# Query, key and value projection of a decoder layer as three rounded passes with two new helpers on VectorE and GpSimd

## The chip, the cores and the metric

The kernel runs on one core of a Trainium2 chip. The metric is device time in microseconds for one launch. The kernel is written without a scheduler: each engine's queue is written out by hand, and the engines meet at semaphores.

## The reference, cut to what matters

A post-norm decoder layer on 128 x 64 tokens of width 128, in three blocks, then a mixture-of-experts block. The change touches the first:

```python
Xn  = _layernorm(X, ln_g, ln_b)
QKV = jnp.einsum('bsd,ed->bse', Xn, W_in)        # 128 -> 384
Q, K, V = jnp.split(QKV, 3, axis=-1)
Q, K = _rotary(Q, ROT), _rotary(K, ROT)
A = jnp.sum(_l2norm(K) * V, axis=-2)
Y = jnp.einsum('bsd,ed->bse', A[:, None, :] * _l2norm(Q), W_out)
# x = _layernorm(x + Y + X); then cross attention with 16 heads of 64,
# layer norm, top-2 routing over 8 experts, expert FFN, layer norm
```

## The kernel before

The 8192 tokens are 64 tiles of 128 rows. The program has three stages: a prologue that prepares weights and takes the first five tiles through the projection, a loop of periods in which all blocks up to the routing run interleaved (period `t` scores tile `t`, projects tile `t+5`, and finishes tiles `t-1` to `t-5`), and then the expert FFN and the closing norm, which don't change.

A period has four units, `k` = 0 to 3. The order of every engine in a unit is written by hand in the function `period` of that engine; waits on semaphores do the rest. In each unit TensorE scores one (batch, half of the heads) pair (L1367), ScalarE takes exponentials (L698) after VectorE has found the maxima (L945), VectorE inverts the sums (L951), GpSimd scales the probabilities (L513), and one unit later TensorE turns them (L1390), ScalarE rounds them (L707), VectorE takes the rests (L956), and TensorE weighs (L1401 to L1404) in three passes of the rounded type `float32r`: high x high, high x low, low x high.

The projection of tile `t+5` goes through these steps, in units 1 and 2 of a period:

- VectorE normalises the rows, `x_hat` (L863);
- TensorE turns them into PSUM, `turn_x` (L1427, unit 1, into columns 384 to 511 of the bank `ps_a`);
- ScalarE applies gain and bias on the way out of PSUM, `x_turned` (L657), giving `xnT`, 128 x 128 in float32;
- TensorE multiplies, `make_qkv` (L1431, unit 2): one float32 instruction of 384 columns, `xnT` stationary and `winT` moving. The profile shows a float32 matmul as two records, a `float32r` matmul as one;
- ScalarE copies the result out, `keep_qkv` (L664), and squares queries and keys (L666), GpSimd makes the inverse roots (`qk_rstds`, L505 and L507), and VectorE rotates (L875 to L885) and multiplies keys by values (L893), after which TensorE turns the queries (L1436).

In the prologue the same functions stand in a written sequence for tiles 0 to 4 between the weight jobs `prepare(0)` to `prepare(14)` (L1348 to L1355); tiles 0 to 4 alternate between `ps_a` and `ps_o`. `winT` is made once by ScalarE (L645) out of the bank `ps_s[0]`, columns 0 to 383; columns 384 to 511 there become `woutT` (L646).

GpSimd's queue in unit 1 is: scale (L513), `ctx_hat` (L546), `latent_hat` (L552), and the indirect DMA that routes rows of an earlier tile (L525); unit 2 begins with the next scale.

Of the kernel before, what the change touches and what calls it, by code (L numbers as in the profile page):

```python
# [14 lines left out]
def decoder_layer(nc, x, ctx_in, w_in, w_out, ln_g, ln_b, ln1_g, ln1_b, ln2_g, ln2_b,  # L15
                  w_q, w_kv, w_o, expert_w, w_g, b_g, rot_cos, rot_sin, batch_of, eye,
                  before, expert_ids, region_base, row_ids, tile_ids, x_rows, y_rows, out):
    F32 = mybir.dt.float32
# [8 lines left out]
    P = 128  # L27
# [35 lines left out]
    with ctx:  # L63
# [20 lines left out]
        b_lat = sb("b_lat", [P, 1])  # L84
        winT = sb("winT", [P, 3 * D])
        woutT = sb("woutT", [P, D])
# [23 lines left out]
        c_hat = sb("c_hat", [P, 2, D])  # L110
        xnT = sb("xnT", [P, 2, D])
        qkv = sb("qkv", [P, 2, 3 * D])
# [161 lines left out]
        def U_BANK(n):  # L274
# [18 lines left out]
        c_in = [sem(f"c_in{q}") for q in range(X_RING)]  # L293
        names = """in_stats in_moments in_eps in_rstd x_hat_done c_hat_done xT_ps xnT_done qkv_ps qkv_done sq_done
        qk_eps qk_rstd rot_turned rot_cosed rot_done kvp_done pick_done at_ps yT_done wo_ps 
# [6 lines left out]
        e_sum_done e_z_done e_stats e_moments e_eps e_rstd e_nm_done e_out_done""".split()  # L302
        (in_stats, in_moments, in_eps, in_rstd, x_hat_done, c_hat_done, xT_ps, xnT_done, qkv_ps, qkv_done, sq_done,
         qk_eps, qk_rstd, rot_turned, rot_cosed, rot_done, kvp_done, pick_done, at_ps, yT_done, wo_ps, 
# [183 lines left out]
        def _(pool):  # L488
# [49 lines left out]
            def qk_rstds(j):  # L538
                q = j % 2
                rstd(ss_qk[:, q], se_qk[:, q], rs_qk[:, q], eps_l2, sq_done, 2 * j + 2, qk_eps, qk_rstd, j)  # L540

            def ctx_hat(j):
                q = j % 2
                pool.wait_ge(in_rstd, j + 1)
                pool.wait_ge(kvT_ps, count(j - 1))
                nc.gpsimd.tensor_scalar(c_hat[:, q], c_raw[:, j % X_RING], mv_in[:, q, 1, 0:1], rs_in[:, q, 1:2],  # L546
                                        ALU.subtract, ALU.mult).then_inc(c_hat_done, 1)
# [7 lines left out]
            def period(t, c):  # L555
                p = c % 2
                for k in range(UNITS):
# [11 lines left out]
                    if k == 1 and on(t, 4):  # L569
                        latent_hat(t + 4)  # L570
                    if k == 2 and on(t, 5):
                        qk_rstds(t + 5)
# [8 lines left out]
            ctx_hat(0)  # L581
            ctx_hat(1)
            qk_rstds(0)
            qk_rstds(1)
            in_rstds(2)
# [3 lines left out]
            latent_hat(1)  # L589
            in_rstds(3)  # L590
            qk_rstds(2)
            ctx_hat(2)
            ctx_hat(3)
            z1_rstds(2)
# [3 lines left out]
            z1_rstds(3)  # L598
            latent_hat(3)
            ctx_hat(4)  # L600
            qk_rstds(4)
# [29 lines left out]
        def _(act):  # L631
# [8 lines left out]
            def keep_prepared(at):  # L640
# [3 lines left out]
                if kind == "in":  # L644
                    nc.scalar.activation(winT[:], bank[:, 0:3 * D], ACT.Copy).then_inc(win_kept, 1)  # L645
                    nc.scalar.activation(woutT[:], bank[:, 3 * D:4 * D], ACT.Copy, scale=0.5).then_inc(prep_act, 1)  # L646
                elif kind == "t":
                    nc.scalar.activation(dst, bank[:], ACT.Copy).then_inc(prep_act, 1)
                elif kind == "m":
                    nc.scalar.activation(heads_of(g, score_hi[:]), bank[:].rearrange("p (c d) -> p c d", c=4), ACT.Copy,  # L650
                                         scale=QS_SCALE).then_inc(prep_act, 1)
                else:
                    nc.scalar.activation(dst, bank[:].rearrange("p (c d) -> p c d", c=4), ACT.Copy).then_inc(prep_act, 1)

            def x_turned(j):
                act.wait_ge(xT_ps, j + 1)
                nc.scalar.activation(xnT[:, j % 2], A_XT(j), ACT.Identity, scale=gcol[:, 0:1],  # L657
                                     bias=bcol[:, 0:1]).then_inc(xnT_done, 1)
# [169 lines left out]
        def _(dve):  # L828
# [32 lines left out]
            def in_hats(j):  # L861
                dve.wait_ge(in_rstd, j + 1)
                nc.vector.tensor_scalar(x_hat[:, j % 2], x_raw[:, j % X_RING], mv_in[:, j % 2, 0, 0:1], rs_in[:, j % 2, 0:1],  # L863
                                        ALU.subtract, ALU.mult).then_inc(x_hat_done, 1)

            def qk(j):
# [70 lines left out]
            def period(t, c):  # L937
# [165 lines left out]
                if on(t, 0):  # L1103
                    row_max(2)
                if on(t, 2):
                    rows_low(t + 2)
# [62 lines left out]
            keep_prepared(1)  # L1169
            in_hats(1)  # L1170
            dve.wait_ge(s_lat, 64)
            nc.vector.tensor_scalar(g_lat[:], g_lat[:], (1 + EPS_LN) ** -0.5, None, ALU.mult).then_inc(g_lat_set, 1)
# [15 lines left out]
            keep_prepared(8)  # L1188
            stats(3)
            x1_norm(1)  # L1190
            in_hats(3)
            rotate(2)
            keep_prepared(9)
# [15 lines left out]
            residual(3)  # L1209
            rows_low(1)  # L1210
            dve.wait_ge(s_gate, 32)
            dve.wait_ge(s_place, 64)
# [111 lines left out]
        def _(pe):  # L1324
# [104 lines left out]
            def make_qkv(j):  # L1429
                pe.wait_ge(xnT_done, j + 1)  # L1430
                nc.tensor.matmul(A_QKV(j), xnT[:, j % 2], winT[:], start=True, stop=True).then_inc(qkv_ps, 1)  # L1431

# [81 lines left out]
            prepare(1)  # L1514
            pe.wait_ge(win_kept, 1)
            make_qkv(0)
# [176 lines left out]
```

## Time and profile before

| what | us |
|---|---|
| median of 3 runs | 1526.59 (1523.41 to 1527.76) |
| profiled execution | 1525.28 |
| its span | 1523.4 |
| PE busy in the span | 1378.8 |
| ACT busy | 1147.2 |
| DVE busy | 1129.9 |
| POOL busy | 902.7 |

PE is TensorE, ACT ScalarE, DVE VectorE, POOL GpSimd. The profile divides the span in 40 slices; the loop of periods fills most of them, the expert FFN and the closing norm the last ten. A row of the timeline gives an instruction's start and length; lengths of matmuls contain the time through the array, so neighbouring matmuls overlap, and what one costs is read from the distance between starts.

### The profile page before, as it was taken

How to read it: one execution, taken by the hardware profiler on the slowest of the kernel's cores; microseconds unless marked ns; L12 is line 12 of the kernel's file. 1: busy time of each engine (PE TensorE's matmuls, PEld its weight loads, DVE VectorE, ACT ScalarE, POOL GpSimd, SP SyncE). 2: the span in 40 equal slices, each digit the busy share in tenths (PEclk: the TensorE clock that was granted, in tenths of full speed). 3: DMA queues.
4: the chain of work that ended last, by engine and by line, in shares of the span. 5: the costliest groups of instructions: out<-in, count | busy, mean ns of one | idle time of the engine just before them, and what ended most of it. 6: DMA issues, size and time to landing. Idle time of an engine off the chain costs nothing. (4 is left out here: it accounts for less than half of the span.)

```text
span 1523.4 us, 37505 instructions
## 1 busy us (share of the span) xinstructions
PE 1378.8 (91%) x10765; PEld 1291.1 (85%) x10765; DVE 1129.9 (74%) x4170; ACT 1147.2 (75%) x4085; POOL 902.7 (59%) x1233
## 2 busy tenths in 40 slices
PE   6799999999999999999999999999993899999940
PEld 4699999999999999999999999999982889989830
DVE  4467777777777777777777777777765678878765
ACT  3588888888888888888888888888872555555535
POOL 4345666666666666666666666666443355555565
PEclk7899999999999999999999999999997899999975
DMA  3000000000000000000000000000003667777746
GB/s 93 11 9 13 16 17 15 21 16 17 16 17 19 16 17 15 21 16 17 15 17 19 16 17 16 20 13 10 9 10 94 210 213 234 225 213 228 219 150 196
DMA packets 64629, 96.24 MB, mean 63 GB/s; under 512 B 10892, under 2 KB 48786, under 8 KB 64306
## 3 DMA queue, kind: packets, MB, share of 16 engines
q1 hardware_dynamic: 44738, 71.90, 15.8%
q0 software_dynamic: 8896, 16.94, 3.2%
q10 hardware_dynamic: 10800, 5.06, 1.2%
q8 instruction: 90, 1.47, 0.4%
q14 instruction: 105, 0.86, 0.2%
HBM read 71.55 MB, written 23.35 MB: 62 GB/s over the span
## 5 line engine op out<-in xcount | busy, mean ns | idle before, releaser
L698 ACT ACTIVATE probs<-ps_s,neg_max 128x128 f32<-128x128 f32 x1024 | 361.8, 365 | 143.8 <-DVE neg_max L945 138.9
L513 POOL TENSOR_TENSOR probs_n<-probs,inv_sum 128x512 f32<-128x512 f32 x256 | 266.6, 1042 | 207.9 <-DVE inv_sum L951 200.4
L1367 PE MATMUL ps_s<-kvT,u_sb 128*128 128x128 f32 x2048 | 275.0, 277 | 0.8 <-issue 0.8
L1380 PE MATMUL ps_o<-value_w,tT 128*128 128x128 f32 x2048 | 260.3, 275 | 1.9 <-ACT tT L716 1.8
L1367 PEld LDWEIGHTS ps_s<-kvT,u_sb 128*128 128x128 f32 x2048 | 254.2, 191 | 7.5 <-issue 1.0
L1380 PEld LDWEIGHTS ps_o<-value_w,tT 128*128 128x128 f32 x2048 | 244.1, 192 | 2.9 <-ACT tT L716 2.9
L956 DVE TENSOR_TENSOR pT_lo<-ps_pT,pT_hi 128x512 fp32r<-128x512 f32 x256 | 175.5, 685 | 85.5 <-ACT pT_hi L707 85.5
L611 POOL DMA_INDIRECT y_rows<-wvT,f_id x144 | 145.2, 1008 | 152.7 <-DVE wvT L1284 100.8
L698 ACT ACTIVATION_READ_ACCUMULATOR probs<-ps_s,neg_max 128x1 f32 x1024 | 207.8, 203 | 0.0
L945 DVE TENSOR_REDUCE neg_max<-ps_s 128x4 f32<-128x512 f32 x256 | 175.9, 687 | 25.6 <-PE ps_s L1367 20.2
L525 POOL DMA_INDIRECT x_rows<-routed,pos_i x128 | 136.6, 1067 | 86.1 <-DVE pos_i L1052 66.1
L1390 PE MATMUL ps_pT<-ident,probs_n 128*128 128x128 f32 x1024 | 157.6, 276 | 13.3 <-DVE pT_lo L956 8.1
L1419 PE MATMUL ps_u<-lT_hi,score_hi 128*128 128x256 f32 x504 | 164.6, 327 | 0.8 <-DVE lT_lo L932 0.8
L716 ACT ACTIVATE tT<-ps_t 128x512 f32<-128x512 f32 x256 | 160.2, 626 | 2.1 <-PE ps_t L1404 1.9
L690 ACT ACTIVATE u_sb<-ps_u 128x512 f32<-128x512 f32 x252 | 152.6, 606 | 9.9 <-PE ps_u L1421 9.8
L707 ACT ACTIVATE pT_hi<-ps_pT 128x512 fp32r<-128x512 f32 x256 | 157.4, 615 | 0.4 <-PE ps_pT L1390 0.3
L951 DVE RECIPROCAL inv_sum<-sums 128x4 f32<-128x4 f32 x256 | 45.7, 178 | 130.7 <-ACT probs L698 130.7
L1421 PE MATMUL ps_u<-lT_hi,score_lo 128*128 128x256 f32 x504 | 142.4, 283 | 0.0
L1420 PE MATMUL ps_u<-lT_lo,score_hi 128*128 128x256 f32 x504 | 142.3, 282 | 0.0
L1390 PEld LDWEIGHTS ps_pT<-ident,probs_n 128*128 128x128 f32 x1024 | 118.3, 146 | 24.0 <-issue 20.8
L1401 PE MATMUL ps_t<-pT_hi,kv_hi 128*128 128x512 f32 x256 | 134.1, 524 | 1.2 <-ACT tT L716 1.1
L1404 PE MATMUL ps_t<-pT_lo,kv_hi 128*128 128x512 f32 x256 | 101.4, 396 | 0.0
(274 smaller groups left out, 3572.3 us busy)
## 6 DMA issues: line engine op xcount, KB each, us to landing
u_sb<-in_expert_w SPq DMA_DIRECT2D x45, 578.0 KB
tT<-in_expert_w SPq DMA_DIRECT2D x27, 578.0 KB
f_x<-x_rows SPq DMA_DIRECT2D x72, 130.0 KB
tT<-y_rows SPq DMA_DIRECT2D x16, 512.0 KB, 4.7
x_raw<-in_x SPq DMA_DIRECT2D x64, 64.0 KB, 1.8
c_raw<-in_ctx_in SPq DMA_DIRECT2D x64, 64.0 KB, 1.9
out<-u_sb ACTq DMA_DIRECT2D x16, 256.0 KB, 2.4
y_rows<-wvT,f_id POOLq DMA_INDIRECT x144
```

The source lines that it names most:

```text
L513: nc.gpsimd.tensor_tensor(probs_n[:, sl], probs[:, sl], inv_sum[:, sl, :].rearrange("p (u o) -> p u o", o=1).to_broadcast([P, UP, P]), ALU ...
L611: pool.indirect_dma_start(out=y_rows, out_offset=bass.IndirectOffsetOnAxis(ap=f_id[:, q % RING, b:b + 1].bitcast(U32), axis=0), in_=f_y[:, ...
L690: nc.scalar.activation(u_sb[:, pair, :, h:h + 2, :].rearrange("p n h s -> p h n s"), U_BANK(n)[:].rearrange("p (h n s) -> p h n s", h=2, s ...
L698: last = nc.scalar.activation(probs[:, sl, j], ps_s[sl][:, j * P:(j + 1) * P], ACT.Exp, bias=neg_max[:, sl, j:j + 1], accum_out=sums[:, sl ...
L707: nc.scalar.activation(pT_hi[:, ss], ps_pT[:], ACT.Copy).then_inc(pT_hi_done, 1)
L716: nc.scalar.activation(tT[:, pp, hf * HH:(hf + 1) * HH, b * S:(b + 1) * S], ps_t[:].rearrange("p (h q) -> p h q", q=S), ACT.Copy).then_inc ...
L945: nc.vector.tensor_reduce(neg_max[:, sl], ps_s[sl][:].rearrange("p (u k) -> p u k", k=P), axis=AX.X, op=ALU.max, negate=True).then_inc(max ...
L956: nc.vector.tensor_tensor(pT_lo[:, ss], ps_pT[:], pT_hi[:, ss].bitcast(F32), ALU.subtract).then_inc(pT_lo_done, 1)
L1367: last = nc.tensor.matmul(ps_s[sl][:, j * P:(j + 1) * P], u_sb[:, c // 2, BT * p + b, h:h + 2].rearrange("p h s -> p (h s)"), kvT[:, c, 2 ...
L1380: last = nc.tensor.matmul(ps_o[:, 0:D], tT[:, (p + 1) % 2, h], value_w[:, h], start=(h == 0), stop=(h == H - 1))
L1390: last = nc.tensor.transpose(ps_pT[:, j * P:(j + 1) * P], probs_n[:, ss, j], ident[:])
L1419: nc.tensor.matmul(u, score_hi[:, h], l_hi, start=True, stop=False)
```

## The change

`winT` becomes two tiles of the rounded type, `winT_hi` (ScalarE, as before) and `winT_lo` (VectorE, the difference between the PSUM bank and `winT_hi`, once). `xnT` becomes `xnT_hi` (ScalarE, as before, rounded on writing) and `xnT_lo`. For the latter VectorE applies gain and bias to the same PSUM columns once more in float32 (`x_full`, into `xn_full`), and GpSimd subtracts (`x_low`). `make_qkv` becomes three instructions of 384 columns: high x high, high x low, and, after a wait for `xnT_lo_done`, low x high.

```diff
+            def x_low(j):                                     # GpSimd
+                q = j % 2
+                pool.wait_ge(xn_full_done, j + 1)
+                pool.wait_ge(xnT_done, j + 1)
+                nc.gpsimd.tensor_tensor(xnT_lo[:, q], xn_full[:, q], xnT_hi[:, q].bitcast(F32), ALU.subtract).then_inc(xnT_lo_done, 1)
...
                     if k == 1 and on(t, 4):
                         latent_hat(t + 4)
+                    if k == 1 and on(t, 5):
+                        x_low(t + 5)
...
             ctx_hat(1)
+            x_low(0)
             qk_rstds(0)
+            x_low(1)
             qk_rstds(1)
...
-                    nc.scalar.activation(winT[:], bank[:, 0:3 * D], ACT.Copy).then_inc(win_kept, 1)
+                    nc.scalar.activation(winT_hi[:], bank[:, 0:3 * D], ACT.Copy).then_inc(win_kept, 1)
...
+            def x_full(j):                                    # VectorE
+                dve.wait_ge(xnT_done, j + 1)
+                nc.vector.tensor_scalar(xn_full[:, j % 2], A_XT(j), gcol[:, 0:1], bcol[:, 0:1],
+                                        ALU.mult, ALU.add).then_inc(xn_full_done, 1)
...
                 if on(t, 0):
                     row_max(2)
+                if on(t, 5):
+                    x_full(t + 5)
                 if on(t, 2):
                     rows_low(t + 2)
...
             in_hats(1)
+            dve.wait_ge(s_norm, 32)
+            x_full(0)
+            dve.wait_ge(prep_act, 1)
+            nc.vector.tensor_tensor(winT_lo[:], banks[0][:, 0:3 * D], winT_hi[:].bitcast(F32), ALU.subtract).then_inc(win_kept, 1)
+            x_full(1)
...
             def make_qkv(j):
-                pe.wait_ge(xnT_done, j + 1)
-                nc.tensor.matmul(A_QKV(j), xnT[:, j % 2], winT[:], start=True, stop=True).then_inc(qkv_ps, 1)
+                pe.wait_ge(xn_full_done, j + 1)
+                nc.tensor.matmul(A_QKV(j), xnT_hi[:, j % 2], winT_hi[:], start=True, stop=False)
+                nc.tensor.matmul(A_QKV(j), xnT_hi[:, j % 2], winT_lo[:], start=False, stop=False)
+                pe.wait_ge(xnT_lo_done, j + 1)
+                nc.tensor.matmul(A_QKV(j), xnT_lo[:, j % 2], winT_hi[:], start=False, stop=True).then_inc(qkv_ps, 1)
...
             prepare(1)
-            pe.wait_ge(win_kept, 1)
+            pe.wait_ge(win_kept, 2)
             make_qkv(0)
```

VectorE's prologue, from the second `x_hat` on: of before,

```order
L863 TENSOR_SCALAR x_hat<-x_raw,mv_in,rs_in 128x128
L1172 TENSOR_SCALAR g_lat<-g_lat 128x1
L844 COPY wkT<-ps_b 128x512
L875 TENSOR_TENSOR turned<-qkv,sinb 128x64 x2
L880 TENSOR_TENSOR qkv<-qkv,cosb 128x2x64
```

and of the change, whose line numbers are its own:

```order
L879 TENSOR_SCALAR x_hat<-x_raw,mv_in,rs_in 128x128
L884 TENSOR_SCALAR xn_full<-ps_a,gcol,bcol 128x128
L1197 TENSOR_TENSOR winT_lo<-ps_s,winT_hi 128x384
L884 TENSOR_SCALAR xn_full<-ps_o,gcol,bcol 128x128
L1200 TENSOR_SCALAR g_lat<-g_lat 128x1
L860 COPY wkT<-ps_b 128x512
L896 TENSOR_TENSOR turned<-qkv,sinb 128x64 x2
L901 TENSOR_TENSOR qkv<-qkv,cosb 128x2x64
```

Three instructions come ahead of the copy of `wkT` and of tile 0's rotation; the third, of tile 1, reads what TensorE turns after tile 0's projection.

GpSimd's prologue, from the second inverse root of the inputs on: of before,

```order
L507 TENSOR_TENSOR rs_in<-ve_in,m_half 128x2
L546 TENSOR_SCALAR c_hat<-c_raw,mv_in,rs_in 128x128 x2
L505 TENSOR_TENSOR se_qk<-ss_qk,eps_l 128x2
L507 TENSOR_TENSOR rs_qk<-se_qk,m_half 128x2
L505 TENSOR_TENSOR se_qk<-ss_qk,eps_l 128x2
L507 TENSOR_TENSOR rs_qk<-se_qk,m_half 128x2
```

and of the change:

```order
L510 TENSOR_TENSOR rs_in<-ve_in,m_half 128x2
L555 TENSOR_SCALAR c_hat<-c_raw,mv_in,rs_in 128x128 x2
L549 TENSOR_TENSOR xnT_lo<-xn_full,xnT_hi 128x128
L508 TENSOR_TENSOR se_qk<-ss_qk,eps_l 128x2
L510 TENSOR_TENSOR rs_qk<-se_qk,m_half 128x2
L549 TENSOR_TENSOR xnT_lo<-xn_full,xnT_hi 128x128
L508 TENSOR_TENSOR se_qk<-ss_qk,eps_l 128x2
L510 TENSOR_TENSOR rs_qk<-se_qk,m_half 128x2
```

Tile 1's rests stand behind tile 0's inverse roots, which need tile 0's squares.

TensorE in unit 2 of a period in the loop: of before,

```order
L1380 MATMUL ps_o<-value_w,tT 128x128 x3
L1490 MATMUL ps_b<-seen,ones 128x8
L1491 MATMUL ps_b<-mask,tri_bf 128x8
L1431 MATMUL ps_a<-winT,xnT 128x384
L1401 MATMUL ps_t<-pT_hi,kv_hi 128x512
L1402 MATMUL ps_t<-pT_hi,kv_lo 128x512
```

and of the change:

```order
L1411 MATMUL ps_o<-value_w,tT 128x128 x3
L1524 MATMUL ps_b<-seen,ones 128x8
L1525 MATMUL ps_b<-mask,tri_bf 128x8
L1462 MATMUL ps_a<-winT_hi,xnT_hi 128x384
L1463 MATMUL ps_a<-winT_lo,xnT_hi 128x384
L1465 MATMUL ps_a<-winT_hi,xnT_lo 128x384
L1432 MATMUL ps_t<-pT_hi,kv_hi 128x512
L1433 MATMUL ps_t<-pT_hi,kv_lo 128x512
```

One row becomes three at the same place, between the bf16 matmuls of the routing and the weighing.

## Rows read from the trace of the kernel before

**Rows 1.** The page: busy time by engine, and the granted TensorE clock in 40 slices.

```profile
PE 1378.8 (91%) x10765; PEld 1291.1 (85%) x10765; DVE 1129.9 (74%) x4170; ACT 1147.2 (75%) x4085; POOL 902.7 (59%) x1233
...
PEclk7899999999999999999999999999997899999975
```

**Rows 2.** Busy time in one stretch of the loop; columns as its heading says.

```profile
core 0: us, PE busy (x) PEld busy (x) DVE busy (x) ACT busy (x) POOL busy (x), PEclk, DMA share, GB/s
140.00:1064.00 924.00, 913.59 (x7180) 856.21 (x7179) 724.87 (x2806) 806.81 (x3076) 606.09 (x864) 1.00 0.06 17
```

**Rows 3.** Waits of PE in that stretch: total us, times, longest.

```profile
PE ps_pT L1390 <- DVE pT_lo L956: 6.6, 27, 0.7
```

**Rows 4.** Timeline of TensorE in one period: start, length, instruction.

```profile
511.36 0.47 PE L1401 MATMUL ps_t<-pT_hi,kv_hi 128*128 128x512 f32 x1
511.67 0.39 PE L1402 MATMUL ps_t<-pT_hi,kv_lo 128*128 128x512 f32 x1
...
513.47 0.28 PE L1420 MATMUL ps_u<-lT_lo,score_hi 128*128 128x256 f32 x1
513.59 0.28 PE L1421 MATMUL ps_u<-lT_hi,score_lo 128*128 128x256 f32 x1
...
515.23 0.89 PE L1431 MATMUL ps_a<-winT,xnT 128*128 128x384 f32 x2
515.66 0.69 PE L1401 MATMUL ps_t<-pT_hi,kv_hi 128*128 128x512 f32 x1
516.18 0.40 PE L1402 MATMUL ps_t<-pT_hi,kv_lo 128*128 128x512 f32 x1
516.42 0.40 PE L1404 MATMUL ps_t<-pT_lo,kv_hi 128*128 128x512 f32 x1
...
518.26 0.60 PE L1390 MATMUL ps_pT<-ident,probs_n 128*128 128x128 f32 x4
```

**Rows 5.** Timeline of VectorE, the same period; idle time before in brackets.

```profile
513.55 0.69 DVE L945 TENSOR_REDUCE neg_max<-ps_s 128x4 f32<-128x512 f32 x1
514.16 0.42 DVE L925 TENSOR_TENSOR kv_lo<-ps_b,kv_hi 128x256 fp32r<-128x256 f32 x1
...
515.81 0.18 DVE L951 RECIPROCAL inv_sum<-sums 128x4 f32<-128x4 f32 x1 [1.09 <-ACT probs L698]
...
517.75 0.69 DVE L945 TENSOR_REDUCE neg_max<-ps_s 128x4 f32<-128x512 f32 x1 [0.26 <-PE ps_s L1367]
```

**Rows 6.** Timeline of ScalarE, the same period.

```profile
513.36 0.49 ACT L657 ACTIVATE xnT<-ps_a,bcol,gcol 128x128 f32<-128x128 f32 x1
```

**Rows 7.** Timeline of GpSimd, the same period.

```profile
513.89 0.78 POOL L552 TENSOR_SCALAR l_hat<-z,mv_z,rs_z 128x128 f32<-128x128 f32 x1
514.85 1.09 POOL L525 DMA_INDIRECT x_rows<-routed,pos_i  x1 [0.18 <-issue]
516.08 1.03 POOL L513 TENSOR_TENSOR probs_n<-probs,inv_sum 128x512 f32<-128x512 f32 x1
```

**Rows 8.** A wider GpSimd group: line, min/median/max ns, first and last start.

```profile
L621 POOL TENSOR_TENSOR u_sb<-tT x16: 712/728/897, 1472.4 to 1511.6; 128x256 f32<-128x256 f32 x16
```

**Rows 9.** Timeline of TensorE in the prologue.

```profile
13.45 1.62 PE L1431 MATMUL ps_a<-winT,xnT 128*128 128x384 f32 x2
14.86 1.04 PE L1348 MATMUL ps_pT<-ident,wq_raw 128*128 128x128 f32 x4
...
17.68 0.60 PE L1348 MATMUL ps_t<-ident,wkv_raw 128*128 128x128 f32 x4
...
55.18 0.91 PE L1431 MATMUL ps_a<-winT,xnT 128*128 128x384 f32 x2 [0.49 <-ACT xnT L657]
```

**Rows 10.** Timeline of VectorE and of GpSimd in the prologue.

```profile
14.24 0.46 DVE L863 TENSOR_SCALAR x_hat<-x_raw,mv_in,rs_in 128x128 f32<-128x128 f32 x1
...
18.18 0.77 POOL L507 TENSOR_TENSOR rs_qk<-se_qk,m_half 128x2 f32<-128x2 f32 x1
```

**Rows 11.** Timelines of GpSimd and of VectorE, unit 3 of the period before.

```profile
503.17 1.04 POOL L513 TENSOR_TENSOR probs_n<-probs,inv_sum 128x512 f32<-128x512 f32 x1 [1.54 <-DVE inv_sum L951]
...
503.27 0.96 DVE L1014 TENSOR_TENSOR mask<-picked 128x8 bf16<-128x8 f32 x1
```

More of the change, by code:

```diff
@@ L84, in decoder_layer @@
         b_lat = sb("b_lat", [P, 1])
-        winT = sb("winT", [P, 3 * D])
+        winT_hi = sb("winT_hi", [P, 3 * D], F32R)
+        winT_lo = sb("winT_lo", [P, 3 * D], F32R)
         woutT = sb("woutT", [P, D])
@@ L110, in decoder_layer @@
         c_hat = sb("c_hat", [P, 2, D])
-        xnT = sb("xnT", [P, 2, D])
+        xn_full = sb("xn_full", [P, 2, D])
+        xnT_hi = sb("xnT_hi", [P, 2, D], F32R)
+        xnT_lo = sb("xnT_lo", [P, 2, D], F32R)
         qkv = sb("qkv", [P, 2, 3 * D])
@@ L293, in decoder_layer @@
         c_in = [sem(f"c_in{q}") for q in range(X_RING)]
-        names = """in_stats in_moments in_eps in_rstd x_hat_done c_hat_done xT_ps xnT_done qkv_ps qkv_done sq_done
+        names = """in_stats in_moments in_eps in_rstd x_hat_done c_hat_done xT_ps xnT_done xn_full_done xnT_lo_done qkv_ps qkv_done sq_done
         qk_eps qk_rstd rot_turned rot_cosed rot_done kvp_done pick_done at_ps yT_done wo_ps
@@ L302, in decoder_layer @@
         e_sum_done e_z_done e_stats e_moments e_eps e_rstd e_nm_done e_out_done""".split()
-        (in_stats, in_moments, in_eps, in_rstd, x_hat_done, c_hat_done, xT_ps, xnT_done, qkv_ps, qkv_done, sq_done,
+        (in_stats, in_moments, in_eps, in_rstd, x_hat_done, c_hat_done, xT_ps, xnT_done, xn_full_done, xnT_lo_done, qkv_ps, qkv_done, sq_done,
          qk_eps, qk_rstd, rot_turned, rot_cosed, rot_done, kvp_done, pick_done, at_ps, yT_done, wo_ps,
@@ L590, in _ @@
             in_rstds(3)
+            x_low(2)
             qk_rstds(2)
             ctx_hat(2)
+            x_low(3)
             ctx_hat(3)
@@ L599, in _ @@
             latent_hat(3)
+            x_low(4)
             ctx_hat(4)
@@ L656, in x_turned @@
                 act.wait_ge(xT_ps, j + 1)
-                nc.scalar.activation(xnT[:, j % 2], A_XT(j), ACT.Identity, scale=gcol[:, 0:1],
+                nc.scalar.activation(xnT_hi[:, j % 2], A_XT(j), ACT.Identity, scale=gcol[:, 0:1],
                                      bias=bcol[:, 0:1]).then_inc(xnT_done, 1)
@@ L1189, in _ @@
             stats(3)
+            x_full(2)
             x1_norm(1)
             in_hats(3)
+            x_full(3)
             rotate(2)
@@ L1210, in _ @@
             rows_low(1)
+            x_full(4)
             dve.wait_ge(s_gate, 32)
```

## The prediction

> **What bounds the kernel now.** I read the page first, then one long stretch of the loop by engine, then TensorE's waits there, and then the timelines of one period on four engines. The page shows TensorE busy for 91% of the span and the granted clock at nine tenths or more from the third slice to the end of the loop, so at its upper level, 2.4 GHz; only the first two slices, the prologue, stand at 0.7 and 0.8, a mixture of both levels [rows 1]. From 140 to 1064 us TensorE is busy 913.59 of 924 us, 98.9% [rows 2], and all of its listed waiting there, 6.6 us, is for one VectorE result [rows 3]. So in the loop a microsecond taken from TensorE should be a microsecond of the program, as long as nothing else is late by as much. The projection stands in unit 2, where TensorE runs without a gap from before 511.36 to after 518.26 [rows 4], and VectorE's last maximum of the period starts at 517.75 after an idle 0.26 us in which it waited for TensorE's scores [rows 5]. Those 0.26 us are how far the engines that TensorE does not drive stand behind it here: a gain up to 0.26 us a period can pass through, more cannot.
>
> The prologue is different: there a chain runs from engine to engine through tile 0's and tile 1's projections, and TensorE's own work stands in fixed order behind it [rows 9, 10]. Work added to the chain is late for everyone.
>
> **The loop, TensorE.** 59 of the 64 tiles are projected in the loop. From the start of the float32 projection, 515.23, to the second weighing pass, 516.18, are 0.95 us; this is the projection and the first weighing pass [rows 4]. A weighing pass of 512 columns takes 516.42 - 516.18 = 0.24, or 0.31 as the first of its run (511.36 to 511.67) [rows 4]. Taking the 0.31, the projection costs 0.64 us. Its two records have 384 columns each, so 0.64 is two cycles a column at 2.4 GHz for each of them. A rounded pass takes one cycle a column and little more: 256 columns in 513.59 - 513.47 = 0.12, 512 in 0.24 [rows 4], so 384 columns take 0.177, between them, and three take 0.53. That is 0.11 less than 0.64. The extra 0.07 of a run's first pass is paid now at L1401 and would be paid at the first of the three passes instead, so I count it as even. It could be paid twice, which leaves 0.04, or, since the three come behind bf16 matmuls and the weighing then comes behind rounded ones, not at all, which makes 0.18. I take 0.11, since two widths on both sides of 384 give it. Over 59 tiles that is -6.5 us, with ends at -2.4 and -10.6.
>
> The Trainium skill (TensorE: Matmul & The Clock Gate, Wait — 56ns, not 53.3ns?) puts back-to-back matmuls at columns over 2.4 GHz plus about 2.5 ns. The trace stays above that: 0.12 against 0.109 us for 256 columns, 0.24 against 0.216 for 512 [rows 4]. By the page three passes would take 0.49 and the loop would gain 8.9 us; I stay with the rows.
>
> **The loop, the two helpers.** ScalarE ends the turned rows at 513.36 + 0.49 = 513.85 [rows 6]. VectorE starts the maximum at 513.55 and the following instruction at 514.16 [rows 5]; `x_full` goes in there. Its length is not shown; a VectorE operation of the same form and size takes 0.46 [rows 10], a 256-wide one out of PSUM 0.42 [rows 5], so about 0.4 at most, and it ends near 514.5. It pushes L925 and what follows by 0.3 us into an idle time of 1.09 us before 515.81 [rows 5], so VectorE pays nothing. The reader of `kv_lo` is a later tile's weighing. `x_low` follows GpSimd's `l_hat`, which ends at 514.67 [rows 7]. Its length: 128x256 takes 0.73 [rows 8] and 128x512 1.03 [rows 7], so about 0.5 for 128x128; the one-input form of this size took 0.78 [rows 7], the upper bound. It ends at 515.2, at worst at 515.45. TensorE wants it for the third pass at 515.23 + 2 x 0.177 = 515.58. So the new wait is met with 0.1 to 0.4 us to spare.
>
> Behind `x_low` in GpSimd's queue are the indirect DMA (514.85, 1.09 long) and the scale at 516.08 [rows 7]. Both slip: the DMA to 515.35 and the scale to about 516.55, 0.5 late, ending at 517.6. Its reader is TensorE's turn at 518.26 [rows 4], which has 0.6 us left, 0.5 once TensorE is faster. If that cover went, the slip would cost its excess each period. The rows that the DMA sends are read after the loop, and its buffer is filled again two periods later.
>
> The Trainium skill (SBUF — State Buffer, Who interferes with whom) says that a VectorE operation with two SBUF inputs and a GpSimd operation that reads SBUF exclude each other for the whole instruction. By that rule, the trace agrees: an eight-column mask on VectorE, 503.27 to 504.23, ends with the 128x512 scale that began at 503.17 and ended at 504.21 [rows 11]. Beside the new GpSimd operation stands `kv_lo`, with one input in PSUM, so the rule would change nothing at this place as planned; it is the ground of the second rival.
>
> **The prologue.** The first projection starts at 13.45 and its successor at 14.86 [rows 9], 1.41 us at the lower level, 1.2 GHz. Now it must wait for `winT_lo`. VectorE's second `x_hat` runs 14.24 to 14.70 [rows 10]; then come `x_full(0)`, to about 15.0, and `winT_lo`, 384 columns out of PSUM, between the 0.42 of 256 and the 0.69 of 512 columns [rows 5], say 0.5. TensorE starts at 15.5, 2.0 us late. Three passes at half the clock take 1.1 instead of 1.41, so what follows is 1.7 late.
>
> Tile 1's third pass waits for `x_low(1)`, which stands behind tile 0's inverse root on GpSimd. That root ends now at 18.18 + 0.77 = 18.95 [rows 10], then at 20.65; with 0.5 for `x_low` it is 21.15, and the last pass lets `prepare(4)` start at about 21.4. It started at 17.68 [rows 9]. So TensorE is 3.7 us late from there, and since its own work stands in order behind this point, and the VectorE and GpSimd chain with it, I let all 3.7 us through. It could be as little as 1.7, if later gaps take up tile 1's part, and as much as 6, if the idle TensorE is granted the lower level longer (the prologue's mixed clock [rows 1]).
>
> For tiles 2 and 3 the third pass waits some tenths, but three passes at the lower level save 0.3 each: zero. Tile 4's projection at 55.18 already waits 0.49 for ScalarE [rows 9], and now for `x_full` and `x_low` too: 0.4 + 0.5, of which 0.45 lies beside the first two passes, so +0.45. I allow as much for the first period, before the rhythm has settled. Sum of the prologue: 3.7 + 0.45 + 0.45 = +4.6 us, with ends at +2 and +7.5.
>
> **The sum.** -6.5 + 4.6 = -1.9 us on the profiled execution: 1525.28 becomes 1523.4. The median of the runs lies 1.3 above the profiled execution, so 1524.7, and I say 1525. All terms at their good ends give 1526.6 - 10.6 + 2 = 1518; all at their bad ends 1526.6 - 2.4 + 7.5 = 1531.7.
>
> **The rivals.**
> First, the full TensorE gain: no first-pass extra in unit 2 at all, 0.18 x 59 = -10.6, with the prologue at +4.6 or less. It gives 1526.6 - 6 = 1520.6, faster. For it: L1401's record starts 0.43 us after the projection's first though the projection costs 0.64 [rows 4], so the starts here don't show where the extra lies. Against it: each run of rounded passes in the loop now shows the extra once.
>
> Second, slower: GpSimd's rest comes too late every period. If `x_low` has to sit out `kv_lo` (0.42) and then takes 0.78, it ends at 514.67 + 0.42 + 0.78 = 515.87, 0.29 after TensorE wants it. The period loses 0.29 and gains 0.11: +0.18 x 59 = +10.6, and with the prologue +15, so 1542. It decides as soon as `x_low` ends after 515.58. Against it: the bounds above end at 515.45, and `kv_lo` has an input in PSUM.
>
> Third, slower: the prologue takes more than the loop gives. With the low end of the loop, -2.4, and 7 us or more lost ahead of the first period, +5, so 1531.5. For it: TensorE idles some 4 us more in a stretch where its clock is mixed.
>
> Fourth, the period does not shorten since VectorE and ScalarE set it: 0 in the loop, +4.6, so 1531. For it: TensorE does wait for VectorE's `pT_lo` [rows 3]. Against it: that VectorE work itself starts from scores that unit 2 sends, and 0.26 us of room are seen [rows 5].
>
> **How the numbers follow.** What a measurement of this kernel can tell from no change is about 0.3%, 4.6 us. My forecast, 1525, has 0.6; the full gain 0.19; the late rest 0.06; the dear prologue 0.08; the unchanged period 0.07. The forecast's own range is 1520 to 1530. Of its 0.6, all but 0.05 lies within 0.3% of before, 0.03 below and 0.02 above. The first rival is mostly faster (0.16 of 0.19), the late rest slower, and half of the other two slower (0.075). So faster is 0.19, slower 0.16, same 0.65. The range 1519 to 1532 leaves out the late rest and the far ends of the others, under 0.2.
>
> **What would show it.** In the profile after: three records of the projection per tile, the third starting about 0.35 us behind the first and not waiting; a period of 0.11 us less between two tiles' projections; an idle time before L951 in unit 2 smaller by 0.3; the scale behind the indirect DMA 0.5 later, and no wait of the turn for it. In the prologue: the first projection at 15.5, the second's last pass near 21.2, the first scores some 4 us later. I am wrong if TensorE lists a wait for the rests in the loop, if the period is unchanged or gains over 0.2, or if the first scores start under 2 or over 8 us later.

## The result and the profile after

The changed kernel has a median of 1518.82 us over nine runs (1514.06 to 1524.34), the kernel before beside it 1527.16 over nine (1523.41 to 1532.04). The ratio is 0.9945 with a 95% interval of 0.9925 to 0.9965: 8.4 us faster, with 5.3 and 11.5 as the ends. The forecast was 1525, no change that can be measured, in a range from 1519 to 1532. The forecast was wrong, and the range missed the median by 0.18 us.

The profiled execution of the changed kernel took 1521.52 us, its span is 1519.7. Against the profile before (1525.28, span 1523.4) that is only 3.8 us less. The rest of the 8.4 lies in which executions were profiled: this one was 2.7 above its kernel's median, the one before 1.9 below its own. A second profile of each kernel has spans of 1525.5 and 1518.5, 7.0 apart. Both pairs are used below. Ratios compare fast executions alone; one execution of one experiment, `helpers_only`, was slow at 2974.67 us, so its periods are read from a second run of the same kernel, `helpers_again`.

The page after, busy time by engine and the granted clock:

```profile
PE 1375.9 (91%) x10829; PEld 1304.0 (86%) x10829; DVE 1147.2 (75%) x4235; ACT 1148.0 (76%) x4085; POOL 934.1 (61%) x1297
...
PEclk9999999999999999999999999999997899999975
```

The same stretch of the loop as in [rows 2], by engine:

```profile
140.00:1064.00 924.00, 915.32 (x7304) 871.24 (x7304) 746.84 (x2881) 816.05 (x3109) 639.39 (x927) 1.00 0.06 17
```

VectorE and GpSimd work 22 and 33 us more there, mostly the two helpers, and TensorE is busy for as much of it as before. The wait that answers to [rows 3]:

```profile
PE ps_pT L1421 <- DVE pT_lo L977: 7.6, 44, 0.2
```

It is still TensorE's only listed wait from 140 to 1056 us; none is for the new helpers. It now comes 44 times with at most 0.2 us, where it came 27 times with up to 0.7. That change of pattern was the first hint, and a part of it stood in the rows of before: of the 6.6 us there, 3.2 lie in only five waits of 0.51 to 0.70 us, one in each of five long periods.

TensorE around the projection, and four projections in a row (start, length, instruction):

```profile
315.29 0.42 PE L1462 MATMUL ps_a<-winT_hi,xnT_hi 128*128 128x384 f32 x1
315.55 0.34 PE L1463 MATMUL ps_a<-winT_lo,xnT_hi 128*128 128x384 f32 x1
315.72 0.34 PE L1465 MATMUL ps_a<-winT_hi,xnT_lo 128*128 128x384 f32 x1
315.90 0.39 PE L1432 MATMUL ps_t<-pT_hi,kv_hi 128*128 128x512 f32 x1
316.12 0.40 PE L1433 MATMUL ps_t<-pT_hi,kv_lo 128*128 128x512 f32 x1
...
332.26 0.42 PE L1462 MATMUL ps_a<-winT_hi,xnT_hi 128*128 128x384 f32 x1
...
348.87 0.42 PE L1462 MATMUL ps_a<-winT_hi,xnT_hi 128*128 128x384 f32 x1
...
365.85 0.42 PE L1462 MATMUL ps_a<-winT_hi,xnT_hi 128*128 128x384 f32 x1
```

Projection and first weighing pass take 316.12 - 315.29 = 0.83 us, where they took 0.95 [rows 4]. The periods are 16.97, 16.61 and 16.98: the middle one is odd. All of them, listed for both kernels from the starts of L1431 and L1462, show a steady period and a few odd ones:

| profile | steady period | odd periods |
|---|---|---|
| before | 17.085 | 17.45, 17.64, 17.62, 17.64, 17.54 |
| before, second | 17.10 | 17.47, 17.66, 17.63, 17.65, 17.55 |
| after | 16.97 | 16.61, 16.61, 16.64 |
| after, second | 16.97 | 16.63, 16.62, 16.63 |

The odd ones stand at the same tiles in both profiles of a kernel. Before, each is long, five together +2.5 us; after, each is short, three together -1.05 us. That makes 3.5 us between the kernels, on top of the steady 0.115 to 0.13. Two or three periods among the first four of the loop are shorter in all four profiles (16.3 to 16.7) and are left out of the table.

| part, us | first pair | second pair | forecast |
|---|---|---|---|
| to TensorE's turn of tile 5's rows | 68.31 to 75.39: +7.1 | 68.51 to 73.69: +5.2 | +4.6 |
| from there to the turn of tile 63's | 992.2 to 982.6: -9.6 | 993.0 to 981.9: -11.1 | -6.5 |
| the rest, to the end of the span | -1.2 | -1.1 | 0 |
| span | -3.7 | -7.0 | -1.9 |

### The profile page after: what moved, and what is told of

Its sections match the earlier page's. It is cut to its first block, busy times and chain, and to the rows that moved or that the text cites. A ratio compares the mean times of both kernels' runs of the same rounds, so it can differ in the third digit from the quotient of the medians.

```text
span 1519.7 us, 37827 instructions
## 1 busy us (share of the span) xinstructions
PE 1375.9 (91%) x10829; PEld 1304.0 (86%) x10829; DVE 1147.2 (75%) x4235; ACT 1148.0 (76%) x4085; POOL 934.1 (61%) x1297
## 4 chain that ended last, share of the span: by engine, by line
PE 42%; DVE 20%; issue 18%; ACT 11%; DMA 5%; SPq 2%; POOL 1%; ACTq 0%; DVEq 0%; POOLq 0%
ACT probs L714 9%; PE ps_s L1398 8%; DVE neg_max L966 6%; PE ps_pT L1421 4%; DVE pT_lo L977 4%; PE ps_o L1411 4%; PE ps_t L1635 3%; DVE mask L1035 3%; PE ps_u L1635 3%; DMA f_x<-x_rows 2%; PE ps_t L1433 2%; PE ps_t L1435 2%; PE ps_t L1432 2%; DMA out<-u_sb 1%; PE ps_u L1450 1%
## 5 line engine op out<-in xcount | busy, mean ns | idle before, releaser
L1432 PE MATMUL ps_t<-pT_hi,kv_hi 128*128 128x512 f32 x256 | 116.6, 455 | 1.2 <-ACT tT L732 1.1
```

Source lines behind the costliest of these rows:

```text
L1432: nc.tensor.matmul(ps_t[:], kv_hi[:, own, b], pT_hi[:, ss], start=True, stop=False)
```

## Why a period is long, steady or short

A steady period after, VectorE and then GpSimd:

```profile
325.26 0.91 DVE L1042 TENSOR_TENSOR seen<-seen,mask 128x8 bf16<-128x8 bf16 x1
```
```profile
325.12 1.03 POOL L516 TENSOR_TENSOR probs_n<-probs,inv_sum 128x512 f32<-128x512 f32 x1
```

An addition of eight columns takes VectorE 0.91 us while GpSimd scales the probabilities. VectorE ends with GpSimd: 326.17 and 326.15. Behind the addition stands VectorE's maximum of unit 1. A short period, the one that ends at 348.87, same two engines:

```profile
342.23 0.15 DVE L1042 TENSOR_TENSOR seen<-seen,mask 128x8 bf16<-128x8 bf16 x1
```
```profile
341.43 0.18 POOL L508 TENSOR_TENSOR ve_z<-mv_z,eps_ln 128x1 f32<-128x1 f32 x1 [1.08 <-DVE mv_z L993]
...
342.40 1.03 POOL L516 TENSOR_TENSOR probs_n<-probs,inv_sum 128x512 f32<-128x512 f32 x1
```

Against the preceding projection the addition stands where it stood (9.97 us behind it in both), but the scale comes at 10.14 instead of 9.83, and the addition gets through in 0.15. The period is 0.36 shorter. TensorE's turn in unit 1, which waits in the steady period, waits for nothing in the short one:

```profile
325.88 1.95 PE L1411 MATMUL ps_o<-value_w,tT 128*128 128x128 f32 x16
328.01 0.63 PE L1421 MATMUL ps_pT<-ident,probs_n 128*128 128x128 f32 x4 [0.18 <-DVE pT_lo L977]
...
342.86 1.95 PE L1411 MATMUL ps_o<-value_w,tT 128*128 128x128 f32 x16
344.64 0.60 PE L1421 MATMUL ps_pT<-ident,probs_n 128*128 128x128 f32 x4
```

The turn starts 2.13 us behind the 16 matmuls ahead of it in the steady period and 1.78 behind them in the short one. So 0.35 us are lost, nearly the whole difference between the periods, but the profile lists only 0.18 of it as waiting: the group's recorded length, 1.95 in both, covers the other half. A busy share near 100% therefore doesn't show that TensorE has no wait.

A long period of the kernel before, the one that starts at 515.23, VectorE:

```profile
525.10 0.29 DVE L1031 COPY routed<-rows 128x256 f32<-128x256 f32 x1 [0.23 <-issue]
525.30 1.00 DVE L1033 COPY routed<-rids 128x2 int32<-128x2 int32 x1
526.22 0.34 DVE L906 SCALAR_TENSOR_TENSOR z<-ps_a,rs_qk,x_raw 128x128 f32<-128x128 f32 x1
526.48 0.15 DVE L1021 TENSOR_TENSOR seen<-seen,mask 128x8 bf16<-128x8 bf16 x1
```

Here VectorE pauses for 0.23 us in which it waits for nothing that the profile shows. The copy behind the pause, two columns wide, starts beside the scale and takes 1.00 us, and only then come `z` and the addition, so the period is 17.62, 0.53 longer than the steady one. Four of the five long periods of before are of this kind (the copy takes 1.00 to 1.10). The first, 17.45, has its pause directly ahead of VectorE's maximum of unit 1, with the copy and the addition as in a steady period. In other periods such a pause falls where it does no harm, or ahead of the statistics whose result GpSimd waits for before the scale (`mv_z`), where it delays the scale and makes the period short: in all three short periods of after, and in the five of `pad_before` below, the addition takes 0.15 to 0.16.

The Trainium skill (SBUF — State Buffer, Who interferes with whom) says that a VectorE operation with two SBUF inputs and a GpSimd operation that reads SBUF exclude each other. For the addition and the scale the traces agree: 0.91 us beside the scale, 0.15 without it. The copy in the long period was held too, 1.00 instead of 0.16. It has one input, so that sentence does not cover it; the same section also names copies, when VectorE reads one tensor through two ports, and no row here shows whether this copy did.

## The experiments

Ratios and medians compare with the kernel before on the same chip. "Loop" is from the turn of tile 5's rows to that of tile 63's, 992.2 and 993.0 before, 982.6 and 981.9 after.

| run | median, before beside it | ratio (95%) | steady period | odd periods | loop |
|---|---|---|---|---|---|
| after_again | 1517.3, 1527.26 | 0.992 (0.9906 to 0.9934) | 16.97 | three of 16.63 | 981.9 |
| loop_only | 1514.63, 1527.26 | 0.9914 (0.9893 to 0.9936) | 16.97 | three of 17.32, three of 16.61 | 982.8 |
| prologue_only | 1527.81, 1527.26 | 1.0001 (0.9983 to 1.0018) | 17.10 | five of 16.76, one 17.45 | 989.0 |
| helpers_only | 1522.86, 1526.57 | 0.9986 (0.9972 to 1.0001) | 17.13 | three of 17.48, three of 16.78 | 993.2 |
| passes_only | 1527.16, 1534.96 | 0.994 (0.9917 to 0.9962) | 16.97 | six of 17.32 to 17.55, one 16.63 | 985.8 |
| pad_before | 1522.07, 1526.57 | 0.9983 (0.9966 to 1.0) | 17.09 | five of 16.76, two of 17.44 | 989.1 |
| seen_before | 1506.72, 1526.57 | 0.9876 (0.9855 to 0.9897) | 16.77 | three of 17.62 to 17.74 | 975.0 |
| seen_after | 1498.41, 1526.57 | 0.9832 (0.9807 to 0.9856) | 16.61 to 16.64 | none | 964.2 |
| seen_loop | 1506.62, 1534.96 | 0.9818 (0.9797 to 0.9839) | 16.63 | four of 17.5 | 967.8 |
| seen_mask_loop | 1507.03, 1534.96 | 0.9812 (0.9792 to 0.9832) | 16.61 | four of 17.47 | 967.4 |

### Both kernels once more

No edit. The first question was whether the odd periods belong to the program or to one execution.

> The changed kernel once more, for a second profile and more runs. The first profile had 17.09 us per period before and 16.97 after, but also five periods before that were 0.4 to 0.6 longer and three after that were 0.36 shorter. Theory A (these odd periods come from the instruction stream itself, where each engine's queue is fetched, and so belong to each program): the three short periods stand at the same tiles again and the loop is 9 to 10 us shorter than before. Theory B (they are chance): other places and other numbers of them, and the loop gains 6.8 plus or minus 3. Both expect the first scores 4 to 6 us later than before, and the runs' median 5 to 11 us under before.

> The kernel before once more, for its profile alone. Theory A: the long periods (17.4 to 17.6 us) stand again between the same tiles. Theory B: elsewhere, or fewer or more.

They belong to the program: same tiles, same kinds, same sizes, in the second profile of each. Two projections after and two before, one odd period in each pair (second profiles):

```profile
330.05 0.42 PE L1462 MATMUL ps_a<-winT_hi,xnT_hi 128*128 128x384 f32 x1
...
346.68 0.42 PE L1462 MATMUL ps_a<-winT_hi,xnT_hi 128*128 128x384 f32 x1
```
```profile
361.40 0.89 PE L1431 MATMUL ps_a<-winT,xnT 128*128 128x384 f32 x2
...
379.06 0.89 PE L1431 MATMUL ps_a<-winT,xnT 128*128 128x384 f32 x2
```

16.63 and 17.66 us. The loop gained more than the 9 to 10 us expected (11.1), and TensorE's first scores came later than the 4 to 6 expected: they start at 67.60 after and at 60.90 before, 6.7 apart, and at 67.81 and 62.22 in the first profiles, 5.6 apart.

### The loop alone and the prologue alone

`loop_only` keeps the float32 projection for tiles 0 to 4 and makes `winT_lo` late in the prologue; `prologue_only` is the opposite (three passes for tiles 0 to 4, float32 from tile 5).

```diff
             def make_qkv(j):
+                if j < FILL:
+                    pe.wait_ge(xnT_done, j + 1)
+                    nc.tensor.matmul(A_QKV(j), xnT[:, j % 2], winT[:], start=True, stop=True).then_inc(qkv_ps, 1)
+                    return
```

> Three rounded passes for the 59 tiles of the loop alone; tiles 0 to 4 projected in float32 as before, winT_lo made late in the prologue. If the prologue costs what the first profile shows (first scores 5.6 us late), this is 5 to 6 us faster than the whole change, 13 us or so under before (ratio 0.991). If the prologue's loss were taken back later, it would equal the whole change (0.9945).

> The other half: three rounded passes for tiles 0 to 4 alone, float32 in the loop. The theory of the two terms: 4.5 to 6 us slower than before (ratio 1.003 to 1.004), first scores 4 to 6 us late, periods of 17.09. The rival, that the late start costs little since TensorE's clock or later gaps give it back: within 2 us of before.

`loop_only` gains 9.3 to 10.1 us of loop at a steady period of 16.97, and its tile 5 is turned at 67.63, within 0.9 of before. Its ratio came as expected, but its median, 1514.63, is only 2.7 below that of the whole change beside it (1517.3), not 5 to 6: its turn of tile 5 is 6.1 earlier, and its loop 0.9 longer, with three long periods that the whole change does not have. `prologue_only` loses 5 us ahead of the loop (73.44), but its median is still that of before, so the expected 4.5 to 6 us did not show: the 17.10 of its steady periods is that of before, but its odd periods are now short where they were long, and give 3 to 4 us back. The rival's number came true without its reason. So part of what one would book as "the prologue costs little" is luck with the odd periods.

### The helpers alone and the passes alone

`helpers_only` has both helpers from tile 5 on and a single float32 projection that waits for them; `passes_only` has the three passes without the helpers, the third multiplying `xnT_hi` once more, so it leaves out the rests. Both stand on `loop_only`.

```diff
-                nc.tensor.matmul(A_QKV(j), xnT_hi[:, j % 2], winT_hi[:], start=True, stop=False)
-                nc.tensor.matmul(A_QKV(j), xnT_hi[:, j % 2], winT_lo[:], start=False, stop=False)
                 pe.wait_ge(xnT_lo_done, j + 1 - FILL)
-                nc.tensor.matmul(A_QKV(j), xnT_lo[:, j % 2], winT_hi[:], start=False, stop=True).then_inc(qkv_ps, 1)
+                nc.tensor.matmul(A_QKV(j), xn_full[:, j % 2], winT[:], start=True, stop=True).then_inc(qkv_ps, 1)
```
```diff
-                nc.tensor.matmul(A_QKV(j), xnT_lo[:, j % 2], winT_hi[:], start=False, stop=True).then_inc(qkv_ps, 1)
+                nc.tensor.matmul(A_QKV(j), xnT_hi[:, j % 2], winT_hi[:], start=False, stop=True).then_inc(qkv_ps, 1)
```

> In the loop VectorE and GpSimd do their two new operations and TensorE waits for both, but multiplies in one float32 instruction as before; the prologue is that of before. If the gain is TensorE's passes, the period is 17.09 as before, and apart from odd periods the time is that of before. If the helpers themselves bring something (by moving the scale of unit 2), the period is shorter than 17.09; if they cost, longer, and the passes would have brought more than 0.12.

> The helpers with the float32 projection once more, for its profile, since the first one fell into a stretch in which the chip ran at well under its usual speed. Expected as there: period 17.09 if the helpers are free.

> In the loop three rounded passes, but none of the two helpers: the third pass multiplies the high part by winT_hi once more (so the rests of the rows are left out of the result and their product replaced). Prologue as before. If the passes are the whole of the steady gain, the normal period is 16.97 here too, as with the helpers; if the helpers cost something, it is less than 16.97. Odd periods may fall elsewhere, worth up to 4 us either way.

The one execution of `helpers_again` took 1533.09 us, on the chip where before has 1534.96. The passes alone have the steady period of the whole change, 16.97: the helpers add nothing to three passes. Beside a float32 projection they cost 0.03 to 0.045 (17.13 against 17.085 and 17.10; before has no profile on that chip). Each has its own odd periods:

```profile
329.99 0.88 PE L1472 MATMUL ps_a<-winT,xn_full 128*128 128x384 f32 x2
...
346.77 0.88 PE L1472 MATMUL ps_a<-winT,xn_full 128*128 128x384 f32 x2
```
```profile
327.09 0.42 PE L1468 MATMUL ps_a<-winT_hi,xnT_hi 128*128 128x384 f32 x1
...
344.41 0.42 PE L1468 MATMUL ps_a<-winT_hi,xnT_hi 128*128 128x384 f32 x1
```

A short one (16.78) in a slower loop and a long one (17.32) in a faster one. More telling are `loop_only` and `helpers_again`: they give VectorE the same instructions and TensorE different ones, they ran on two chips, and their odd periods end at the projections of the same six tiles (19, 21, 35, 37, 51, 53, counted from 0), each of the same kind. So in this pair the odd periods go with VectorE's instructions, not with TensorE's work or the chip.

### Six instructions at the start

If the odd periods follow from where an instruction stands in VectorE's stream, instructions that do nothing for the loop must move them. `pad_before` is the kernel before with six memsets of eight values, once, at VectorE's start:

```diff
             nc.vector.memset(ones_row[:], 1.0).then_inc(pad_ready, 1)
+            for i in range(6):
+                nc.vector.memset(spare[:, i * E:(i + 1) * E], 1.0)
```

> The kernel before with six VectorE memsets of eight values more at its start, where VectorE idles for 3 us, so that every later VectorE instruction stands six places further on in its stream. Theory (odd periods are made where the stream is fetched): normal periods 17.09 to 17.10 as before, but the odd ones stand elsewhere or turn from long (17.5) to short (16.75) as in the prologue-only kernel; the loop then is 989 instead of 992.6 us. Rival (the odd periods belong to the work, not to the stream): the same five long periods at the same tiles, and the time of before.

Four projections, of this kernel and of before:

```profile
342.94 0.89 PE L1434 MATMUL ps_a<-winT,xnT 128*128 128x384 f32 x2
...
360.03 0.89 PE L1434 MATMUL ps_a<-winT,xnT 128*128 128x384 f32 x2
...
376.79 0.89 PE L1434 MATMUL ps_a<-winT,xnT 128*128 128x384 f32 x2
...
393.89 0.89 PE L1434 MATMUL ps_a<-winT,xnT 128*128 128x384 f32 x2
```
```profile
343.83 0.89 PE L1431 MATMUL ps_a<-winT,xnT 128*128 128x384 f32 x2
...
360.91 0.89 PE L1431 MATMUL ps_a<-winT,xnT 128*128 128x384 f32 x2
...
378.55 0.89 PE L1431 MATMUL ps_a<-winT,xnT 128*128 128x384 f32 x2
...
395.63 0.89 PE L1431 MATMUL ps_a<-winT,xnT 128*128 128x384 f32 x2
```

The middle period goes from 17.64 to 16.76, its neighbours stay within 0.02. Four of the five periods that were long are now short, a fifth short one stands two periods behind the first that was long, and two new long ones stand late in the loop. The loop becomes 3.1 us shorter (992.2 to 989.1). The median stands 4.5 below that of before beside it, but the ratio of 0.9983 is just about no change (upper end 1.0), so the loop of the profile shows it and the time does so only weakly. Padding also shifts nothing else of note: tile 5 is turned at 68.00 (68.31 and 68.51 before). `prologue_only`, on another chip, also puts six VectorE instructions more ahead of the loop (five `x_full` and `winT_lo`), and it has short periods at the same four places and a long one at the same place as the last of `pad_before`.

### The addition moved

If the addition into `seen` is what the steady period pays for, the period must get shorter when the addition goes where GpSimd doesn't scale: ahead of `inverse_sum(0)`, since the scale waits for that inverse.

```diff
                 if on(t, -2):
                     z2_mean()
+                if on(t, -4):
+                    seen_add()
                 if on(t, 0):
                     inverse_sum(0)
...
                 if on(t, 4):
                     z1_sum(t + 4)
-                if on(t, -4):
-                    seen_add()
```

> The kernel before with one VectorE instruction (the eight-column add of seen and mask, two SBUF inputs) moved from behind z1_sum to ahead of the first inv_sum of the period, where GpSimd is idle. Theory: in normal periods this add is held 0.76 us by GpSimd's scale and TensorE's turn in unit 1 waits for it; the odd short periods are those in which it escapes. Then every period is 16.7 to 16.8 and the kernel 19 to 21 us faster (ratio 0.987). Rival: the wait has another cause and the period stays 17.09.

> The same move in the changed kernel. Theory: every period is 16.6 as the three short ones were, 59 x 0.36 = 21 us faster than the change, 28 to 31 under before (ratio 0.981), with fewer odd periods since the race of the two engines is gone. Rival as for the kernel before: 16.97 a period.

The changed kernel with this edit, VectorE and then GpSimd:

```profile
516.33 0.17 DVE L1042 TENSOR_TENSOR seen<-seen,mask 128x8 bf16<-128x8 bf16 x1
516.71 0.18 DVE L972 RECIPROCAL inv_sum<-sums 128x4 f32<-128x4 f32 x1 [0.21 <-ACT probs L714]
```
```profile
517.33 1.03 POOL L516 TENSOR_TENSOR probs_n<-probs,inv_sum 128x512 f32<-128x512 f32 x1
```

and its engines from 140 to 1030 us:

```profile
140.00:1030.00 890.00, 890.00 (x7174) 854.63 (x7173) 701.51 (x2836) 800.37 (x3054) 632.08 (x909) 1.00 0.06 17
```

The addition takes 0.17, TensorE is busy all of the 890 us and lists no wait in that stretch, and every period is a short one. The kernel before gains 0.315 a period with the same edit (17.085 to 16.77), more than TensorE's whole idle time in its loop, 10.4 us in 54 periods or 0.19 a period [rows 2]. `seen_after` has the largest gain in time of all that were run on its chip, 1498.41 against 1526.57.

### The best of both, and one more addition

`seen_loop` joins `seen_add` to `loop_only`, so it keeps the old prologue; `seen_mask_loop` also moves the eight-column `mask` of [rows 11] from beside the scale of unit 3 to ahead of `inverse_sum(3)`.

```diff
+                if on(t, -3):
+                    gate_mask()
                 if on(t, 0):
                     inverse_sum(3)
...
-                if on(t, -3):
-                    gate_mask()
```

> The best version that the runs point to: rounded passes in the loop alone (first scores at 61.5 instead of 67.6) and the eight-column add ahead of the first inv_sum. Theory: the sum of both, 1498.4 - 5 = 1493, ratio 0.979.

> The same and the mask add of unit 3 moved too, from behind the position sums to ahead of the last inv_sum, so that it is not held 0.8 us by GpSimd's last scale of the period. If VectorE's work there is on the path (its maximum of the next period starts 0.1 us after TensorE's scores), up to 0.1 us a period more, 6 us; if TensorE alone sets the period by now, the same 1493.

On this chip the two reach 0.982 and 0.981 of before, short of the 0.979 expected, and on the other `seen_after` reached 0.983; the intervals overlap, so no order among the three is shown. The old prologue's gain (tile 5 turned at 67.93 against 72.26) goes against four long periods that `seen_after` does not have; in each of them the two-column copy is held again, 1.01 us. Moving the mask gives nothing (1507.03 against 1506.62): it was held as long as the addition, but in `seen_loop` TensorE lists only four waits from 140 to 1030 us, those of the long periods, and the steady period falls by no more than 0.02.

## Why the prediction missed

**What bounds the loop: half right.** What was taken from TensorE did shorten the period. But 98.9% busy and 6.6 us of listed waiting were read as all the waiting there is. Behind the addition TensorE waits about 0.35 us in every steady period, half of it inside the recorded lengths, and moving that one VectorE instruction gave 0.315 us a period without touching TensorE.

**Passes in the loop: right.** Forecast 0.11 us a tile; the steady period fell by 0.115 (0.13 in the second pair), and `passes_only` has the whole of it. The third pass started 0.43 behind the first, not 0.35: the first of the run takes 0.26, so the extra for a run's first pass is paid here and no longer at the first weighing pass (0.22). It is paid once, as the sum had it. The first rival, a gain of 0.18 a tile, did not occur, though the measured time stands near its number.

**Helpers in the loop: right.** No wait of TensorE for `xn_full` or `xnT_lo` there, and 16.97 with and without the helpers. VectorE and GpSimd around the projection at 315.29:

```profile
314.22 0.40 DVE L884 TENSOR_SCALAR xn_full<-ps_a,gcol,bcol 128x128 f32<-128x128 f32 x1
...
315.88 0.18 DVE L972 RECIPROCAL inv_sum<-sums 128x4 f32<-128x4 f32 x1 [0.78 <-ACT probs L714]
```
```profile
314.73 0.45 POOL L549 TENSOR_TENSOR xnT_lo<-xn_full,xnT_hi 128x128 fp32r<-128x128 f32 x1
315.60 1.09 POOL L528 DMA_INDIRECT x_rows<-routed,pos_i  x1 [0.42 <-issue]
316.73 1.05 POOL L516 TENSOR_TENSOR probs_n<-probs,inv_sum 128x512 f32<-128x512 f32 x1
```

`x_full` took 0.40 (forecast about 0.4) and `x_low` 0.45 (0.5). `x_low` ended at 315.18, 0.54 ahead of the third pass. VectorE's idle time fell from 1.09 to 0.78, and the scale stands 1.44 behind the projection's start where it stood 0.85 [rows 4, 7], 0.6 later against 0.5 forecast, still without a wait of the turn. The late rest, the slower rival, did not occur.

**Prologue: mechanism right up to tile 1, size too low behind it.** TensorE and GpSimd there:

```profile
15.26 0.69 PE L1462 MATMUL ps_a<-winT_hi,xnT_hi 128*128 128x384 f32 x1 [1.82 <-DVE winT_lo L1197]
...
20.88 0.69 PE L1465 MATMUL ps_o<-winT_hi,xnT_lo 128*128 128x384 f32 x1 [0.95 <-POOL xnT_lo L549]
21.36 1.05 PE L1379 MATMUL ps_t<-ident,wkv_raw 128*128 128x128 f32 x4
```
```profile
20.36 0.46 POOL L549 TENSOR_TENSOR xnT_lo<-xn_full,xnT_hi 128x128 fp32r<-128x128 f32 x1
```

The first projection came at 15.26 (forecast 15.5), tile 1's last pass at 20.88 (21.15), `prepare(4)` at 21.36 (21.4), 3.7 late as forecast (4.2 in the second pair). But the first scores were 5.6 and 6.7 us late against "some 4". Two things are seen on the way. The four matmuls of `prepare(4)` took 1.05 us where they took 0.60 [rows 9], so TensorE stood at the lower level, 1.2 GHz, for longer, which the prediction had as its bad end; at the turn of tile 2's rows the delay was 5.2 and 5.1. And tile 2, put at zero, cost 0.44: it took 3.04 us from its turn to the next where it took 2.60, waiting 0.99 for `x_full` where it had waited 0.55 for ScalarE.

From the first scores to tile 5's turn the granted level was a matter of luck, and in the two pairs it fell in opposite ways. Eight matmuls of the first scores, in the first and second profile before, then in the first and second after:

```profile
62.22 1.13 PE L1367 MATMUL ps_s<-kvT,u_sb 128*128 128x128 f32 x8 [0.84 <-issue]
```
```profile
60.90 1.71 PE L1367 MATMUL ps_s<-kvT,u_sb 128*128 128x128 f32 x8 [0.84 <-issue]
```
```profile
67.81 2.04 PE L1398 MATMUL ps_s<-kvT,u_sb 128*128 128x128 f32 x8 [0.84 <-issue]
```
```profile
67.60 1.13 PE L1398 MATMUL ps_s<-kvT,u_sb 128*128 128x128 f32 x8 [0.87 <-issue]
```

With 1.13, the upper level, the stretch to tile 5's turn took 6.09 us in either kernel; where the level was lower it took 7.61 before and 7.58 after (granted clock 0.63 from 60 to 65 us and 0.69 from 65 to 70 in that profile before, 0.50 from 70 to 74 in that one after). So 7.1 is too much and 5.2 too little: at equal levels the prologue cost 5.6 and 6.7, 1.0 to 2.1 more than the 4.6 forecast.

**The step that failed: the loop's term of the sum, 59 x 0.11 = -6.5.** It measured -9.6 and -11.1. I read one period of before and multiplied it by 59, as if all were alike. Five were long by 2.5 us in all; after the change none is long and three are short by 1.05. That part, 3.5 us, needs no change of the projection: six spare memsets move as much. With -3.5 the sum would have been -5.4, thus 1526.6 - 5.4 = 1521.2. A list of all 59 projection starts of before shows the five long ones; what they would turn into could not be read from it, and that should have widened the range downward by some 4 us. The sum with every term at its good end, 1518, held the measured time; the range that was stated began 1 us above it. The prologue's miss went the other way, so the time came nearer to the forecast than the loop's term did.

What the profiles show does not reach the whole of the 8.4 us. At equal levels of the clock loop and prologue together take 4.5 us off in the first pair (there the loop's first period after began at the lower level and was 0.5 longer) and 4.4 in the second. The stretch behind tile 63's turn is 1.1 to 1.2 shorter after in both pairs, but the code there is nearly the same, and over four profiles on one chip it measures 461.0 to 466.4 us, so this can be chance. Some 3 us are in no term and stay open; the interval of the gain begins at 5.3.

**Not settled.** That the odd periods depend on which instructions VectorE has, and on six that only stand ahead of the loop, is shown by the padding and by the kernels that share their odd places; that the pauses are made where the stream is fetched is not shown, nor was a rule for where they fall tried. The cost of a period's pause also depends on the neighbours of the instruction that it hits.

## What to carry to other kernels

List the starts of one repeated instruction over the whole loop before multiplying one period by their number; a few odd periods can be worth more than the edit. Look for tiny VectorE operations with two SBUF inputs that take about 1 us beside a GpSimd operation, and move them to where GpSimd idles: one such line was worth 0.31 to 0.36 us a period here, nearly three times the steady gain of the change studied, while another of the same size off the critical path was worth nothing. When an edit adds or removes instructions on VectorE, expect some us of change in either direction that the edit does not explain, and test with a padded version of the old kernel. When two profiles are compared stage by stage, compare stretches in which like matmuls run at the same pace: the clock level alone moved one stretch of 6.09 us by 1.5.

## What was unexpected in the hardware

An addition of eight columns on VectorE took 0.91 us beside a GpSimd scale and 0.15 without it, and a copy of two columns 1.00 instead of 0.16, although it has one input. Of the 0.35 us that TensorE lost behind the addition, the profile listed 0.18 as waiting. Six memsets executed once changed where and of what kind the odd periods of a loop of a thousand microseconds are. And the granted clock of the first slices stands at 9 in the profile after, while three passes of 384 columns start 0.32 apart, which is the lower level's pace (0.17 to 0.18 in the loop):

```profile
15.74 0.52 PE L1463 MATMUL ps_a<-winT_lo,xnT_hi 128*128 128x384 f32 x1
16.06 0.52 PE L1465 MATMUL ps_a<-winT_hi,xnT_lo 128*128 128x384 f32 x1
```

The record of this profile says 1.00 from 28 to 50 us too, while the second profile after, with the same lengths of the same instructions there (2.07 us for eight of L1384), says 0.50. So the spacing of like matmuls is the safer sign of the level.
